# Four pieces of the values stored by the attention stage, two of them computed at its head

## The reference, cut to what matters

```python
q = (x @ Wq.T).reshape(B, L, 32, 128)
k = (x @ Wk.T).reshape(B, L, 8, 128)
v = (x @ Wv.T).reshape(B, L, 8, 128)
q, k = rope(q), rope(k)
dt = softplus(x @ Win.T + dt_bias)
G = cumsum(-dt * exp(A_log_bias))       # within a chunk of 128 tokens
y = (scores * decay) @ (v * dt) + (q * exp(G)) @ state
out = x + (rms_norm(y) * gnorm_w * silu(x @ Wg.T)) @ Wo.T
```

## Time and profile before

| what | us |
| --- | --- |
| median of 3 runs | 1774.86 |
| lowest and highest of them | 1773.87, 1774.93 |
| the profiled execution, its own time | 1773.33 |
| its span in the trace | 1771.5 |
| TensorE busy in the span | 1741.7 (98%) |
| VectorE | 1270.9 (72%) |
| GpSimd | 851.4 (48%) |
| ScalarE | 715.5 (40%) |
| mean granted clock of TensorE | 0.996 of full speed |

### The profile page before, as it was taken

One profiled execution on the slowest core, in us unless ns is written; L12 is line 12 of the kernel. 1 busy time (PEld: TensorE's weight loads), 2 busy tenths in 40 slices (PEclk: granted clock), 3 DMA queues, 4 the chain that ended last, 5 costly groups with the idle time before them and its releaser, 6 DMA issues. The chain is left out here.

```text
span 1771.5 us, 27984 instructions
## 1 busy us (share of the span) xinstructions
PE 1741.7 (98%) x8744; PEld 1469.5 (83%) x8744; DVE 1270.9 (72%) x2353; ACT 715.5 (40%) x2232; POOL 851.4 (48%) x862
## 2 busy tenths in 40 slices
PE   7998999999999999999999999999989999999998
PEld 6787888888888888888888888888878888888886
DVE  5326898988999999999898999998874333333332
ACT  3424444454445444544445444544652111111111
POOL 3225677667757766676766775776501101010101
PEclk9999999999999999999999999999999999999999
DMA  6333323423333333343342333333572323232321
GB/s 203 91 106 100 115 87 99 127 91 107 119 90 114 121 89 96 106 122 87 99 128 93 104 118 92 111 93 111 191 248 79 107 72 107 72 106 72 106 72 47
DMA packets 145985, 190.31 MB, mean 107 GB/s; under 512 B 9136, under 2 KB 79792, under 8 KB 145840
## 3 DMA queue, kind: packets, MB, share of 16 engines
q1 hardware_dynamic: 145840, 188.58, 34.8%
HBM read 141.89 MB, written 46.66 MB: 106 GB/s over the span
## 5 line engine op out<-in xcount | busy, mean ns | idle before, releaser
L114 POOL TENSOR_TENSOR q<-raw_wo_early 128x512 f32<-128x512 f32 x128 | 164.9, 1289 | 202.0 <-DVE raw_wo_early L106 201.5
L85 PE MATMUL p_proj<-shared,wq_hi 128*128 128x512 f32 x744 | 244.5, 390 | 0.0
L1113 ACT ACTIVATE square<-p_y 128x128 f32<-128x128 f32 x512 | 134.6, 278 | 216.4 <-PE p_y L837 216.0
L1846 POOL TENSOR_TENSOR var<-mv,eps 128x1 f32<-128x1 f32 x16 | 3.1, 192 | 403.9 <-DVE mv L1696 403.9
L837 PE MATMUL p_y<-v_tok,probs 128*128 128x128 f32 x1024 | 182.1, 275 | 0.0
L985 DVE SCALAR_TENSOR_TENSOR z<-p_y,srstd,gate 128x128 f32<-128x128 f32 x512 | 143.4, 341 | 48.9 <-issue 31.8
L1088 ACT ACTIVATE probs<-g_row,stab 128x128 f32<-128x128 f32 x512 | 164.3, 406 | 25.2 <-POOL g_row L1214 25.2
L85 PE MATMUL p_kept<-wg_hi,shared 128*128 128x512 f32 x560 | 173.2, 390 | 0.0
L1228 POOL TENSOR_TENSOR xw_lo<-xw_raw,xw_hi 128x512 fp32r<-128x512 f32 x96 | 131.1, 1365 | 86.6 <-ACT xw_hi L1125 86.6
L85 PEld LDWEIGHTS p_proj<-shared,wq_hi 128*128 128x128 f32 x744 | 139.6, 188 | 30.4 <-DVE raw_wo_early L106 1.2
L85 PE MATMUL p_proj<-wg_hi,shared 128*128 128x512 f32 x528 | 162.6, 389 | 0.0
(11 more groups left out here) (239 smaller groups left out, 4402.2 us busy)
## 6 DMA issues: line engine op xcount, KB each, us to landing
g_row<-g_scratch SPq DMA_DIRECT2D x128, 256.0 KB, 4.9
z_scratch<-z_st SPq DMA_DIRECT2D x256, 128.0 KB
w_raw<-z_scratch SPq DMA_DIRECT2D x62, 512.0 KB, 6.5
e_row<-e_scratch SPq DMA_DIRECT2D x96, 256.0 KB, 4.0
w_raw<-in_wq_t SPq DMA_DIRECT2D x16, 512.0 KB, 7.2
w_raw<-in_wg_t SPq DMA_DIRECT2D x16, 512.0 KB, 5.3
v_tok<-v_scratch SPq DMA_DIRECT2D x32, 256.0 KB, 2.9
v_scratch<-n_xin SPq DMA_DIRECT2D x22, 256.0 KB, 2.3
```

Source lines behind the costliest of these rows:

```text
L85: mm = pe.matmul(out, lhs[a], rhs[e], start=(i == 0 and j == 0), stop=(i == len(pairs) - 1 and j == 2))
L114: pool.tensor_tensor(out, keep["rope_a"][:, s, :], keep["rope_b"][:, s, :], ALU.add).then_inc(keep["roped"], 1)
L1113: s = act.activation(square[:, h, :], p_y[c % 2][:, h, :], ACT.Square, scale=2.0 / float(np.sqrt(D)), accum_out=ssum[:, c, h:h + 1])
```

## The change

Two numbers are new: `V_LEFT` = 4 pieces are stored by the attention stage, and `V_LATE` = 2 of them are also made there. The norm stage makes pieces 0 to 29 and saves and stores 0 to 27. The five projections are no longer followed by a piece each: pieces 26 and 27 stand behind the second and the fourth, 28 and 29 behind the fifth.

In the attention stage TensorE's `first()` makes piece 30 into `p_y[0]`, waits until pieces 28 and 29 are saved out of `p_tok` and `p_kept`, turns K, and makes piece 31 into `p_y[1]`. ScalarE makes the high parts of K and of q first, then saves 28 and 29, and then does the rest; 30 and 31 are saved behind `xw_high`. All four go to `q[1]`, the query buffer of step 1. SP stores them between its first loads and that of `gn`. Its wait for these stores moves from step 0 to step 1, and GpSimd's moves from ahead of the first rotation's addition to ahead of the second in step 0. GpSimd makes `xw_raw` ahead of its wait for the row of chunk 1. The second half of the values' weights has to outlive the norm stage, and the order of some tensors in SBUF is changed for that.

```diff
@@ -49,6 +49,9 @@
 T_BIAS, T_W = range(TAB)
 LEAST_DT = 2.0 ** -60
 
+V_LEFT, V_LATE = 4, 2
+V_SAVED, V_MADE = 2 * NT - V_LEFT, 2 * NT - V_LATE
+
 
 def wait_ge(engine, sem, count):
 
@@ -120,7 +123,7 @@
 
     shared, tab, ident, g_dram, e_dram, w_raw, wk, wq, wg = (keep[k] for k in (
         "shared", "tab", "ident", "g_dram", "e_dram", "w_raw", "wk", "wq", "wg"))
-    v_dram, v_out, v_tok = keep["v_dram"], keep["v_out"], keep["v_tok"]
+    v_dram = keep["v_dram"]
     assert B * H == P
     with ExitStack() as ctx:
         def sb(name, shape, dt=F32):
@@ -151,6 +154,7 @@
 
 
         wv = [wg, [sb(f"n_wv_{part_}", [P, KT, GW], F32R) for part_ in ("hi", "lo")]]
+        keep["wv_last"] = wv[1]
         v_rows = [xin[:, i, :] for i in (14, 15)] + [xn[:, i, :] for i in range(2)]
         pt = [pb(f"n_pt{i}", [P, KT, P]) for i in range(2)]
         pdt = pb("n_pdt", [P, L])
@@ -165,7 +169,7 @@
         k_in, q_in, g_in, trig_in = sem("n_k_in"), sem("n_q_in"), sem("n_g_in"), sem("n_trig_in")
         wv_first, wv_in = [sem(f"n_wv_first{i}") for i in range(2)], sem("n_wv_in")
         unit_done, rope_terms, roped = sem("n_unit_done"), keep["rope_terms"], keep["roped"]
-        v_done, v_set = sem("n_v_done"), sem("n_v_set")
+        v_done, v_set = keep["v_done"], keep["v_set"]
         w_hi, w_lo, wv_lo = sem("n_w_hi"), sem("n_w_lo"), sem("n_wv_lo")
         const_set, acol_set = sem("n_const_set"), sem("n_acol_set")
         stats_set, mv_set, var_set, rstd_set, xn_set = (sem(f"n_{n}_set") for n in ("stats", "mv", "var", "rstd", "xn"))
@@ -192,15 +196,13 @@
         TOGETHER = [(0, 1), (1, 2), (2, 4)] + [(b * NC, (b + 1) * NC) for b in range(1, B)]
 
         def v_place(v):
-            if v >= 2 * NT - 2:
-                return (keep["k"][:, 1, :], v_tok[:, 1, :, :].rearrange("p c d -> p (c d)"))[v - (2 * NT - 2)]
             return xin[:, v, :] if v < NT - 2 else v_rows[v % 4]
 
 
         early_out, place_out = sem("n_early_out"), [sem(f"n_place_out{i}") for i in range(4)]
 
         def v_count(v):
-            return early_out if v < NT - 2 else place_out[v % 4] if v < 2 * NT - 2 else v_out
+            return early_out if v < NT - 2 else place_out[v % 4]
 
         @block.sync
         def _(sp):
@@ -246,12 +248,11 @@
             sp.dma_start(g_dram.rearrange("c b g h t -> (b g h) c t"), G[:, :].rearrange("h (c t) -> h c t", t=C)).then_inc(g_out, 16)
             sp.wait_ge(eg_set, 1)
             sp.dma_start(e_dram.rearrange("c b g h t -> (b g h) c t"), eg[:, :].rearrange("h (c t) -> h c t", t=C)).then_inc(g_out, 16)
-            for v in range(NT + TABLES, 2 * NT):
+            for v in range(NT + TABLES, V_SAVED):
                 store_v(v)
             sp.wait_ge(g_out, 32)
-
             for i in range(4):
-                sp.wait_ge(place_out[i], 16 * NT // 4)
+                sp.wait_ge(place_out[i], 16 * sum(v % 4 == i for v in range(NT - 2, V_SAVED)))
 
         @block.gpsimd
         def _(pool):
@@ -395,7 +396,7 @@
 
             def save_v(v):
                 act.wait_ge(v_done, v + 1)
-                if NT + 2 <= v < 2 * NT - 2:
+                if v >= NT + 2:
                     act.wait_ge(place_out[v % 4], 16 * ((v - (NT - 2)) // 4))
                 if v in (NT - 2, NT - 1, NT, NT + 1):
                     act.wait_ge(xt_done, NT)
@@ -450,7 +451,7 @@
             for j, k in enumerate((T_BIAS, T_W)):
                 act.wait_ge(tabs_done, j + 1)
                 act.activation(tab[:, :, k, :], ptab[k][:, :, :], ACT.Copy).then_inc(tabs_saved, 1)
-            for v in range(NT + TABLES_AT, 2 * NT):
+            for v in range(NT + TABLES_AT, V_SAVED):
                 save_v(v)
 
         @block.tensor
@@ -518,10 +519,13 @@
                 values(v)
             for k in (T_BIAS, T_W):
                 turn_table(k)
+            v = NT + TABLES_AT
             for r in range(ROPED):
                 project_tile(r)
-                values(NT + TABLES_AT + r)
-            for v in range(NT + TABLES_AT + ROPED, 2 * NT):
+                if r % 2:
+                    values(v)
+                    v += 1
+            for v in range(v, V_MADE):
                 values(v)
 
 
@@ -552,15 +556,16 @@
         q_part = [sb(f"q_{e}", [P, HG, C], F32R) for e in ("hi", "lo")]
         k_part = [sb(f"k_{e}", [P, L], F32R) for e in ("hi", "lo")]
         qs = sb("qs", [P, HG, C])
-        state = sb("state", [P, 2, HG, D])
-        tanh = sb("tanh", [P, GW])
         gate = sb("gate", [P, 2, GW])
-        square = sb("square", [P, HG, D])
         ssum = sb("ssum", [P, NC, HG])
         svar = sb("svar", [P, NC, HG])
         srstd = sb("srstd", [P, NC, HG])
         mhalf = sb("mhalf", [P, HG])
         eps4 = sb("eps4", [P, HG])
+
+        state = sb("state", [P, 2, HG, D])
+        tanh = sb("tanh", [P, GW])
+        square = sb("square", [P, HG, D])
         z = sb("z", [P, HG, D])
 
         z_st = sb("z_st", [P, 2, TB, HG, NC // 2, BL])
@@ -671,6 +677,10 @@
                 load_g(0, 0, 0)
                 load_g(0, 0, 1)
                 load_e(0, 0, 1)
+                for i in range(V_LEFT):
+                    sp.wait_ge(v_set, V_SAVED + i + 1)
+                    sp.dma_start(v_dram[HG:2 * HG, NT - V_LEFT + i].rearrange("g s d -> s g d"),
+                                 q[1][:, i, :].rearrange("p (g d) -> p g d", g=HG)).then_inc(keep["v_out"], 16)
                 sp.dma_start(keep["gn"][:, :], io["gnorm_w"].rearrange("(p a) -> p a", a=1)).then_inc(keep["gn_in"], 16)
 
             def step(g, b, n):
@@ -685,8 +695,8 @@
                 if ahead(n):
                     if has_last(n):
                         sp.wait_ge(y_done, NC * n)
-                    else:
-                        sp.wait_ge(keep["v_out"], 16 * 2)
+                    if isinstance(n, int) and n == 1:
+                        sp.wait_ge(keep["v_out"], 16 * V_LEFT)
                     load_v(g + (b + 1) // B, (b + 1) % B)
                 for c in range(NC):
 
@@ -825,6 +835,8 @@
 
                 m = NC * n + c
                 wait_ge(pe, z_set, m - 1)
+                if not has_last(n) and c < V_LATE:
+                    pe.wait_ge(v_set, V_MADE + c + 1)
                 if c == 0:
                     pe.wait_ge(v_in[b % 2], v_loads(g, b))
                 else:
@@ -837,8 +849,18 @@
                     mm = pe.matmul(p_y[c % 2][:, h, :], probs[:, c % 2, h, :], v_tok[:, b % 2, c, :], start=(c == 0), stop=True)
                 mm.then_inc(y_done, 1)
 
+            def last_values(i):
+                tile = NT - V_LATE + i
+                wide(pe, p_y[i][:, :, :].rearrange("p h t -> p (h t)"),
+                     [(x_parts(keep, tile // NC, kt, slice(tile % NC * P, (tile % NC + 1) * P)),
+                       [w[:, kt, :] for w in keep["wv_last"]]) for kt in range(KT)]).then_inc(v_done, 1)
+
             def first():
+                last_values(0)
+
+                pe.wait_ge(v_set, V_MADE)
                 k_turn(0, 0)
+                last_values(1)
 
             def straight(first, step):
 
@@ -1119,6 +1141,10 @@
                 wait_ge(act, cst_done, 3 * n)
                 act.activation(k_tok[0][:, :, :], p_tok[:, 0:NC - 1, :], ACT.Copy).then_inc(tok_hi_set, 1)
 
+            def save_last(i, bank_):
+                act.wait_ge(v_done, V_SAVED + i + 1)
+                act.activation(q[1][:, i, :], bank_[:, :, :].rearrange("p h t -> p (h t)"), ACT.Copy).then_inc(v_set, 1)
+
             def xw_high(n, c):
                 act.wait_ge(xw_raw_set, 3 * n + c + 1)
                 wait_ge(act, cst_done, 3 * n + c)
@@ -1126,10 +1152,14 @@
 
             def first():
                 k_high(0, 0)
+                q_high(0, 0, 0)
+                for i in range(V_LEFT - V_LATE):
+                    save_last(i, (p_tok, keep["p_kept"])[i])
                 save_k(0)
-                q_high(0, 0, 0)
                 make_decay(0, 0, 0)
                 xw_high(0, 0)
+                for i in range(V_LATE):
+                    save_last(V_LEFT - V_LATE + i, p_y[i])
 
             def last_step(g, b, n):
                 squares(n - 1, 3)
@@ -1245,9 +1275,9 @@
                 step_tables(0, 0, 0)
                 row_landed(0, 0)
                 mask(0, 0)
+                make_xw(0, 0, 0, 0)
                 row_landed(0, 1)
                 mask(0, 1)
-                make_xw(0, 0, 0, 0)
 
             def step(g, b, n):
                 xw_low(n, 0)
@@ -1259,11 +1289,12 @@
                 xw_low(n, 1)
                 row_landed(n, 2)
                 if ahead(n):
-                    if not has_last(n):
-                        pool.wait_ge(keep["v_out"], 16 * 2)
                     add_rope(pool, keep, n + 1, b + 1, 0)
                 mask(n, 2)
                 if ahead(n):
+                    if not has_last(n):
+
+                        pool.wait_ge(keep["v_out"], 16 * V_LEFT)
                     add_rope(pool, keep, n + 1, b + 1, 1)
                 rms(n, 0)
```

(2 more changed lines are left out.)

## The result

The changed kernel takes 1765.49 us (median of 6 runs, 1764.94 to 1766.36), and the kernel before 1774.58 in the same session (6 runs, 1773.80 to 1775.14). The ratio is 0.9948, with an interval of 0.9937 to 0.9958: 9.1 us or 0.5% faster. The forecast was 1767.3 with a range of 1765.2 to 1770.6, so the time lies at its lower edge: the direction and the case were right, and the gain was 1.5 us larger than the 7.6 worked out.

A forecast was written before the change was run, and what follows sets the result against it. TensorE's matmul work was taken to bound the attention stage, with 8.09 us idle or slow-clock time reachable at its head. Gaining 7.59 gave 1774.86 - 7.6 = 1767.3 us, range 1765.2 to 1770.6.

The forecast's parts named there:

- The change of stage: Norm to attention stage, TensorE now ending last: 0.50 us taken, bounds 0 and 1.66; stage begins 6.92 us earlier.
- Saves ahead of the transposes: Attention head: ScalarE done 2.48 us into the stage, piece 30 covers TensorE to 2.80; cost 0, cover 0.3.
- To the scores: Attention head: 130.74 + 2.80 + 0.32 + 2.80 = 136.66 against 140.09, 3.43 us gained.
- To the first chunk's state: Attention head: xw_lo ends at 139.03, TensorE comes at 140.16, so the state's 147.75 start becomes 140.16.
- rival A: Attention head: second chunk's row lands late, 1.5 to 3.0 us; 1767.7 to 1769.2 us; chance 0.22.
- B: Change of stage: TensorE's code not there, a transfer awaited, 1.9 us over the 0.50; 1769.2 us; chance 0.05.
- C: Attention head: clock falls anyway, scores and K projection cost 2.66 us more; gain 4.9, 1769.9 us; chance 0.06.
- SP's hold: SP held at piece 31's store; third g row issued at about 139.9, landing 146.0; cost 0, cover 5.4 us.
- rival E: Slower: longer landings at the head with SP's hold delay chunk 2's g row; 1782 at 3 times; chance 0.03.
- The sum: Attention head: 7.59 us gained of 8.09 within reach, taken from the earlier kernel's median.
- The accounting of the clock: Attention head: scores and K projection take 3.50 us at full clock in place of 6.16 at the lowered one.
- Rival D: Gain given back at the attention stage's end or in a step meeting a transfer; 1771 to 1775 us; chance 0.07.

The follow-up runs named there:

- e2_two_stored: Changed kernel with only two pieces stored by the attention stage and none made there (V_LEFT 2, V_LATE 0); 1770.23 us, ratio 0.9972 to the kernel before.
- e3_one_late: Changed kernel with three pieces stored by the attention stage, one made there, ahead of the transposes; 1768.05 us, ratio 0.9959 to the kernel before.
- e1_before_again: Kernel before, no edit, run again for a second trace; 1775.04 us, ratio 1.0001.
- e12_before_third: Kernel before, no edit, run last for a third trace; 1775.03 us, ratio 1.0005.
- e5_fill: Kernel before plus 9 matmuls into an unread bank between transposes and scores of the attention stage's head; 1776.04 us, ratio 1.0008.
- e4_order: Kernel before with only the change's order: q_high ahead of save_k, xw_raw ahead of the second row's wait; 1772.65 us, ratio 0.9991.
- e10_fill_both: Kernel before plus 9 unread matmuls between transposes and scores and 15 behind the first step's K projection; 1774.59 us, ratio 0.9998.
- e11_after_again: Changed kernel, no edit, run again for a second trace; 1765.35 us, ratio 0.9948 to the kernel before.

## Why the prediction was right, point by point

**The change of stage.** 0.50 us was taken between bounds of 0 and 1.66. It was 129.82 - 129.33 = 0.49, of which 0.32 is idle.

**Saves ahead of the transposes.** Done 2.1 us into the stage (2.48 taken), with the transposes at 2.87. Without that cover, e2_two_stored shows the price: 2.47 us waited.

**To the scores.** 6.49 us from the last matmul, 6.42 said (0.50 + 2.80 + 0.32 + 2.80).

**To the first chunk's state.** 9.90 us, 9.92 said. xw_lo ended 8.24 us behind SP's first issue of the stage at 129.79 (8.29 said) and 1.2 us ahead of TensorE (1.1 said). The second row landed earlier behind the stage's start than before, in no more than 6.1 us against 6.4, so rival A did not come about. Nor did B: the change of stage with TensorE last took 0.32 us, so the wait for a transfer that the Trainium skill's rule would give ("Runtime: NRT & Kernel Launch", "Instruction fetch mechanics") was not there. Whether this branch is one that its rule means, no run here shows. Nor did C.

**SP's hold.** The third g row went out at 139.96 (139.9 said). That the times agree is luck: counted from the stage's start it went out at 10.2 us and not at 9.2, and the whole stage lay 0.9 us earlier than assumed. It landed in 4.3 us, not 6.1, so the longer landings that rival E needed were not there.

**The sum.** Against the first trace of before the head gained 18.99 - 11.23 = 7.76 us, 7.59 said. What failed is the step from there to the median: "The forecast is for a median, so 1774.86 - 7.6". It took one profiled execution of the kernel before for all of them. That execution was one of its faster ones, 1773.33 in runs of up to 1777. The forecast thus let the changed kernel's median lie 1.5 us above its own trace as well, and it lay 0.2 above (1765.49 against 1765.26). The prediction had kept these 1.5 us in its range. What the median execution of before has more than that trace is not shown. The head is one place for it: the other two traces have 19.36 and 21.42. By the third the head gained 8.13 us and by the second 10.19, and the mean of the three, 8.7 us, is near the 9.1 of the medians. But one of the three is the slowest of its ten runs, so that mean is no estimate of the median; the middle one, 8.1, leaves 1.0 us open. And in the slowest, more of the excess stood behind the head than in it. The opening, a few tenths of a us, is another place. For the other kernels the same means come as near: e3_one_late gained 5.8, 8.3 and 6.2 by head, 6.8 in the mean, and 7.0 in the medians; e2_two_stored 4.6 in the mean and 4.8.

Ten runs of the changed kernel lie within 1.4 us, and ten of before in e1_before_again and in e12_before_third spread over 4.0 and 3.7. But the six of before measured beside the changed kernel spread over 1.3 only, so whether the change also narrows the spread is open.

**The accounting of the clock.** The prediction gave scores and projection at full clock a gain of their own of 2.66 us. By the traces of e12_before_third, e5_fill and e2_two_stored the clock ahead of the state was worth nothing there: a chain from the stage's start over the landing of two rows, masks and xw_lo set the state, and TensorE's speed ahead of it only moved idle time. The sum came out right because the forecast asked what was last at each point, and because the moved pieces pushed TensorE behind that chain. By experiment the 7.8 us of the head are then, in this order and against the first trace of before: 1.4 for the order alone (e4_order; 1.7 and 3.8 against the other two), 2.3 more for handing two saves and stores over the change of stage (e2_two_stored), 2.2 for the first piece made at the head and 1.9 for the second.

**Rival D.** At the mix of the last step's first chunk the changed kernel was 9.17 us ahead (1255.98 against 1265.15), and a part of that is a wait for wq_lo, 0.58 us in the trace of before and 0.30 here. At the end of the span it was 8.1 ahead. In between are the wait for qs, 2.26 us against 1.36, the low clock behind it, 3.39 us for a mix against 1.77, and the wait at the change to the output stage, 1.87 us against 3.38. The first two took back 2.5 us of the lead and the third gave 1.5. So 1.0 us of the lead was given back in this execution, far less than rival D's half, and the low clock is what took it. The changed kernel's second trace has waits of 1.4 and 3.5 there and no low stretch, the first and third of before 1.4 and 3.4, and the second of before 2.3 and 3.8. So either kernel shows either wait, and no run shows it to be a cost of the change; what makes it was not tried.

**Open.** How often an execution of the kernel before has the second low clock was not counted; three traces don't give a frequency. The mean granted clocks on record, 0.994 to 0.997 in 94 runs of the kernel before and 0.997 to 0.999 in ten of the changed one, say that executions differ and not at which place. That mean heads and medians agree within 0.4 us for the changed kernel and its two smaller forms fits a share of the head but does not prove it; for e5_fill they are 0.6 us apart, for e10_fill_both 0.7.

## What to carry to other kernels

When a stage opens with several chains that run side by side (loads, splits, a low clock), ask for each only whether it is the last one; a sum over TensorE's waits counts idle time that the next chain gives back as another wait. Independent work that can be moved behind the meeting of the engines covers all those chains at once, until TensorE is behind the slowest. And compare a forecast from one trace with the run it belongs to. Where that run is at the fast end, do not carry the difference to the median over to the changed kernel unread: it may be part of what the change removes, and only traces of slower executions can say at which place it stands.

## What the runs showed of the hardware that was not expected

A wait of TensorE at full clock can be followed by a low clock that costs 1.6 us more, in some executions and not in others. At the head, waits of 1.97, 2.50 and 4.21 us for xw_lo were followed by 8.7 us from state to scores in place of 7.1; waits of 0.90, 1.33, 1.36 and 1.60 us were not, and in one trace one of 2.92 was not either. In the last step a wait of 2.26 us was followed by a stretch at 0.52 (after), one of 2.25 was not (e1_before_again), and those of 1.35 to 1.38 in the other 12 traces were not. At the change to the output stage 13 traces have a wait of 3.2 to 3.8 us; in 11 the granted clock was down to 0.50 by its end or shortly after, in two (e4_order with 3.32 and e11_after_again with 3.53) it stayed at 1.00. So the length of the wait alone does not decide it. In e10_fill_both 15 matmuls that compute nothing of use, put into such a wait, kept the clock at 1.00, and the kernel was 1.5 us faster than e5_fill in the medians.

The meeting of all engines between two stages left TensorE idle for the same time in each trace in which it was the last to arrive with work waiting on the other side, to the hundredth (0.32 in six traces).
